# Late projections of an attention kernel: from f32 matmuls to three products of f16 terms

## The reference

```python
xn = _layernorm(x)
q = split(xn @ q_w.T + q_b) / sqrt(16); k = split(xn @ k_w.T + k_b); v = split(xn @ v_w.T + v_b)
attn = softmax(q @ k^T)                  # over all 4096 keys, in float32
att  = merge(attn @ v) @ out_w.T + out_b
w_fp8, w_scale = quant_fp8(weight); x_fp8, x_scale = quant_fp8(xn)
ffn  = (x_fp8 @ w_fp8.T * (x_scale * w_scale) + bias).astype(bfloat16)
out  = x + att + ffn
```

## Time and profile before

| | |
|---|---|
| median of three runs | 1831.96 us |
| the profiled execution | 1832.19 us, span 1830.3 us |
| ACT busy | 1734.1 us, 95% |
| PE busy, DVE busy | 1631.1 us, 1622.4 us (89% each) |
| POOL busy | 48.2 us, 3% |
| exponentials on ACT (line 916) | 1856, busy 1711.1 us |
| matmuls of late projections (line 1632) | 128 records, busy 36.2 us |
| granted TensorE clock | 9 tenths or more of full speed in all 40 slices |

### The profile page before, as it was taken

The page is one execution under the profiler, slowest core; times in us unless marked ns, Lnnn a source line. Parts: engine busy times, 40 slices in busy tenths (PEclk is TensorE's granted clock), DMA queues, the critical chain, the costliest instruction groups (busy, mean ns, idle before and its releaser), DMA issues.

```text
span 1830.3 us, 74852 instructions
## 1 busy us (share of the span) xinstructions
PE 1631.1 (89%) x33478; PEld 558.8 (31%) x33478; DVE 1622.4 (89%) x1876; ACT 1734.1 (95%) x1898; POOL 48.2 (3%) x71
## 2 busy tenths in 40 slices
PE   7998999899899889899888889898898989899887
PEld 4532222222222222222222222222222222222224
DVE  8889989899898989989888998989899898989988
ACT  2499999999999999999999999999999999999993
POOL 0000000000000000000000000000000000000000
PEclk9999999999999999999999999999999999999999
DMA  7401111110111111011110101101000100100113
GB/s 206 143 17 39 36 39 39 32 34 14 42 36 34 44 31 26 23 42 36 34 32 16 35 19 30 25 17 33 21 21 15 25 19 16 27 15 15 31 26 113
DMA packets 127081, 68.59 MB, mean 37 GB/s; under 512 B 77792, under 2 KB 117664, under 8 KB 126752
## 3 DMA queue, kind: packets, MB, share of 16 engines
q1 hardware_dynamic: 126272, 63.54, 13.3%
q10 hardware_dynamic: 480, 0.20, 0.0%
HBM read 41.93 MB, written 17.27 MB: 32 GB/s over the span
## 4 chain that ended last, share of the span: by engine, by line
ACT 45%; issue 26%; PE 18%; DVE 9%; DMA 0%; ACTq 0%; SPq 0%; DVEq 0%
ACT probs L916 45%; PE banks L1666 8%; PE banks L1610 4%; DVE bits L1272 2%; PE banks L1632 2%; PE banks L1521 1%; PE banks L1511 1%; DVE horner L1279 1%; DVE horner L1285 1%; DVE powers L1282 1%; DVE d_probs L1290 1%; PE banks L1793 1%; DVE powers L1276 1%; PE banks L1682 0%; ACTq L915 0%
## 5 line engine op out<-in xcount | busy, mean ns | idle before, releaser
L916 ACT ACTIVATE probs<-banks 128x1024 f32<-128x1024 f32 x1856 | 1711.1, 1116 | 12.4 <-PE banks L1610 5.2
L1666 PE MATMUL banks<-probs,v_st 64*32 64x512 f32 x14848 | 971.1, 590 | 0.3 <-DVEq L1254 0.2
L1610 PE MATMUL banks<-q_st,k_st 50*32 50x512 f16 x16384 | 764.7, 381 | 172.5 <-ACT probs L916 158.0
L1610 PEld LDWEIGHTS banks<-q_st,k_st 50*32 50x32 f16 x16384 | 229.9, 89 | 1070.9 <-ACT probs L916 907.5
L1272 DVE TENSOR_SCALAR bits<-banks 128x1024 int32<-128x1024 f32 x192 | 235.0, 1224 | 64.3 <-PE banks L1610 57.6
L1666 PEld LDWEIGHTS banks<-probs,v_st 64*32 64x32 f32 x14848 | 266.2, 106 | 58.4 <-issue 1.4
L1282 DVE SCALAR_TENSOR_TENSOR powers<-powers,horner 128x1024 f32<-128x1024 int32 x192 | 235.7, 1228 | 6.6
L1279 DVE SCALAR_TENSOR_TENSOR horner<-powers 128x1024 f32<-128x1024 int32 x192 | 235.4, 1226 | 6.6
L1285 DVE SCALAR_TENSOR_TENSOR horner<-powers,horner 128x1024 f32<-128x1024 f32 x192 | 235.2, 1225 | 6.6
L1290 DVE SCALAR_TENSOR_TENSOR d_probs<-horner,bits 128x1024 int32<-128x1024 f32 x192 | 235.2, 1225 | 6.6
L1276 DVE TENSOR_SCALAR powers<-bits 128x1024 int32<-128x1024 int32 x192 | 133.3, 694 | 6.6
(11 more groups left out here) (117 smaller groups left out, 460.4 us busy)
## 6 DMA issues: line engine op xcount, KB each, us to landing
late_x<-xnT_copy SPq DMA_DIRECT2D x32, 256.0 KB, 3.3
k_st<-k_parts SPq DMA_DIRECT2D x96, 64.0 KB, 2.3
q_st<-q_parts SPq DMA_DIRECT2D x186, 32.0 KB, 1.9
k_st<-k_parts SPq DMA_DIRECT2D x96, 60.0 KB, 2.2
xnT_copy<-probs SPq DMA_DIRECT2D x8, 512.0 KB, 3.4
q_st<-neg_row SPq DMA_DIRECT2D x256, 1.0 KB, 1.7
w_f<-xnT_copy SPq DMA_DIRECT2D x16, 256.0 KB, 2.9
xn_all<-ctx_out SPq DMA_DIRECT2D x128, 32.0 KB, 2.2
```

Of the source, the lines that this page charges most:

```text
L916: act.activation(probs[:, at:at + WIDE * CHUNK].rearrange("p (t c) -> p t c", t=WIDE), banks[:, bank:bank + WIDE, :], ACT.Exp, bias=EXP_SHIFT,
L1610: last = pe.matmul(banks[cols, bank + g, :], k_st[rows, keys], blocks[rows, j], start=True, stop=True, tile_position=(g * GROUP, t * VCOLS))
L1666: last = pe.matmul(banks[VCOLS * qb:VCOLS * (qb + 1), 6 + half, :], v_st[keys, kt, :], src[keys, g * CHUNK:(g + 1) * CHUNK], start=at == 0 ...
```

## The change

The late projection is made from f16 terms: x = x_high + x_low and w = w_high + w_low, and the product from w_high x_high, w_high x_low and w_low x_high. With two halves of the 256 input features that is six f16 matmuls in place of two f32 ones.

- ACT writes w_high (f16) instead of the f32 copy, and POOL subtracts it from the weights into w_low, once, before its first copy of values.
- `late_x[:, 0]` is now the one staging buffer of the f32 input, and the memory of `late_x[:, 1]` holds its two f16 terms. POOL makes them, per late projection: a conversion of 128x512 into x_high and a subtraction of 128x512 into x_low (`split_late`). It waits for the load and for the late projection before, which reads the same terms.
- SP loads one input at a time, when the split before has emptied the buffer: slot 0 at the end of the unit before, slot 1 behind the rows of maxima of its own unit.
- POOL's loop over heads is written out, with the splits in front of and between the copies of values.

```diff
+        late_in = late_x[:, 0]
+        late_terms = late_x.rearrange("p i k c -> p i (k c)")[:, 1].bitcast(F16).rearrange("p (t k c) -> p t k c", t=PARTS, k=KD)
...
+        LATE_PRODUCTS = ((0, 0), (0, 1), (1, 0))
...
-            def load_late(n):
+            def load_late(n, slot):
-                for slot in range(len(LATE_AT)):
-                    o, chunk, part = late_item(n * len(LATE_AT) + slot)
-                    at = chunk * CHUNK + part * LATE_COLS
-                    sp.dma_start(late_x[:, slot], xnT_dram[:, :, at:at + LATE_COLS]).then_inc(late_x_in[slot], 16)
+                i = n * len(LATE_AT) + slot
...
+                if i:
+                    sp.wait_ge(late_x_split, i)
+                sp.dma_start(late_in, xnT_dram[:, :, at:at + LATE_COLS]).then_inc(late_x_in, 16)
...
                     save_late(n)
-                    if n + 1 < LATE_UNITS:
-                        load_late(n + 1)
+                    load_late(n + 1, 0)
...
                         load_rows(c, 1, h * 2 + 2)
+                        load_late(h * UNITS, 1)
...
                             load_rows(c, 0, h * 2 + 3)
+                        load_late(h * UNITS + 1, 1)
...
+            pool.wait_ge(late_w_ready, 2)
+            for i, name in enumerate("qk"):
+                high, low = late_w_terms[:, i, 0], late_w_terms[:, i, 1]
+                pool.tensor_tensor(low, w_sb[name][:, :, P:2 * P], high, ALU.subtract).then_inc(late_w_split, 1)
...
+            def split_late(n, slot):
+
+                i = n * len(LATE_AT) + slot
...
+                if i:
+                    h, u = divmod((i - 1) // len(LATE_AT), UNITS)
+                    pool.wait_ge(first.st_done, first.place_0(h, u) + LATE_AT[1 - slot] + 1)
+                pool.wait_ge(late_x_in, 16 * (i + 1))
+                pool.tensor_copy(late_terms[:, 0], late_in).then_inc(late_x_high, 1)
+                pool.wait_ge(late_x_high, i + 1)
+                pool.tensor_tensor(late_terms[:, 1], late_in, late_terms[:, 0], ALU.subtract).then_inc(late_x_split, 1)
...
-                with pool.Fori(1, FIRST_EARLY // UNITS + 1) as h:
-                    head_values(c, h)
+                split_late(0, 0)
+                for n in range(FIRST_EARLY):
+                    split_late(n, 1)
+                    if n % UNITS:
+                        next_values(c, n // UNITS + 1, 0)
+                    split_late(n + 1, 0)
+                    if n % UNITS:
+                        next_values(c, n // UNITS + 1, 1)
...
-                        act.activation(late_w[:, i], w_sb[name][:, :, P:2 * P], ACT.Copy).then_inc(late_w_ready, 1)
+                        act.activation(late_w_terms[:, i, 0], w_sb[name][:, :, P:2 * P], ACT.Copy).then_inc(late_w_ready, 1)
...
-                    pe.wait_ge(late_w_ready, 2)
-                    pe.wait_ge(late_x_in[slot], 16 * (n + 1))
-                    for k in range(KD):
-                        x_cols = late_x[:, slot, k, :]
-                        last = pe.matmul(banks[:, bank_at(h, u, p), 0:LATE_COLS], late_w[:, o, k, :],
+                    pe.wait_ge(late_w_split, 2)
+                    pe.wait_ge(late_x_split, n * len(LATE_AT) + slot + 1)
+                    terms = [(w, x, k) for w, x in LATE_PRODUCTS for k in range(KD)]
+                    for w, x, k in terms:
+                        x_cols = late_terms[:, x, k, :]
+                        last = pe.matmul(banks[:, bank_at(h, u, p), 0:LATE_COLS], late_w_terms[:, o, w, k, :],
                                          x_cols if o else x_cols.rearrange("f (i j p) -> f j i p", i=CT // 2, j=QB),
-                                         start=(k == 0), stop=(k == KD - 1))
+                                         start=(w, x, k) == terms[0], stop=(w, x, k) == terms[-1])
```

More of the change, by code:

```diff
@@ L204, in program @@
         late_w = sb("late_w", [P, 2, KD, P])
+        late_in = late_x[:, 0]
+        late_terms = late_x.rearrange("p i k c -> p i (k c)")[:, 1].bitcast(F16).rearrange("p (t k c) -> p t k c", t=PARTS, k=KD)
+        late_w_terms = late_w.rearrange("p i k c -> p i (k c)").bitcast(F16).rearrange("p i (t k c) -> p i t k c", t=PARTS, k=KD)
         rden_rows = late_x.rearrange("p i k c -> p i (k c)")
@@ L241, in program @@
         late_w_ready = sem("late_w_ready")
-        late_x_in = [sem(f"late_x_in{i}") for i in range(len(LATE_AT))]
+        late_w_split = sem("late_w_split")
+        late_x_in = sem("late_x_in")
+        late_x_high = sem("late_x_high")
+        late_x_split = sem("late_x_split")
         late_hi = sem("late_hi")
@@ L656, in _ @@
             sp.wait_ge(xT_saved, 16 * NCH)
-            def load_late(n):
-                for slot in range(len(LATE_AT)):
-                    o, chunk, part = late_item(n * len(LATE_AT) + slot)
-                    at = chunk * CHUNK + part * LATE_COLS
-                    sp.dma_start(late_x[:, slot], xnT_dram[:, :, at:at + LATE_COLS]).then_inc(late_x_in[slot], 16)
+            def load_late(n, slot):
+                i = n * len(LATE_AT) + slot
+                if n >= LATE_UNITS:
+                    return
+                o, chunk, part = late_item(i)
+                at = chunk * CHUNK + part * LATE_COLS
+                if i:
+                    sp.wait_ge(late_x_split, i)
+                sp.dma_start(late_in, xnT_dram[:, :, at:at + LATE_COLS]).then_inc(late_x_in, 16)
             def save_late(n):
@@ L696, in attend @@
                 else:
-                    load_late(0)
+                    load_late(0, 0)
                 for h in range(HEADS):
@@ L809, in _, with next_values @@
             pool.partition_all_reduce(amax_all[:, :], amax[:, :, 7], P, RMAX).then_inc(amax_shared, 1)
+            def next_values(c, h, half):
+                pool.wait_ge(c.pv_done, h * STEPS + (PV_0 - STEPS) + KT + c.summed[half])
+                copy_values(c, h, half)
             def head_values(c, h):
                 for half in range(2):
-                    pool.wait_ge(c.pv_done, h * STEPS + (PV_0 - STEPS) + KT + c.summed[half])
-                    copy_values(c, h, half)
+                    next_values(c, h, half)
+            def split_late(n, slot):
+                i = n * len(LATE_AT) + slot
+                if n >= LATE_UNITS:
+                    return
+                if i:
[5 more added lines that the diff above has]
+                pool.tensor_tensor(late_terms[:, 1], late_in, late_terms[:, 0], ALU.subtract).then_inc(late_x_split, 1)
             def add_early(h, u, slot):
@@ L1287, in d_block @@
                     dve.wait_ge(c.d_chain, steps + D_STEPS)
+                    if not c.full and h == 0 and u == 0 and n == 0:
+                        dve.wait_ge(late_w_split, 2)
                     if n >= 2:
```

## The result

| | median, us | lowest to highest | runs |
|---|---|---|---|
| before | 1832.13 | 1831.79 to 1833.54 | 5 |
| changed | 1841.25 | 1839.30 to 1842.92 | 5 |

The ratio is 1.0049, with a 95% interval of 1.0035 to 1.0064: the change makes the kernel slower, by 9.1 us. The forecast was 1836.0. The profiled execution of the changed kernel took 1841.14 us (span 1839.3), 9.0 more than that of before.

What follows compares the result with a forecast made beforehand. ACT's own pace was taken as the bound (95% busy). 1832.19 - 9.0 (PE) + 12.8 (POOL's splits) + 0.3 (weights' subtractions) = 1836.3 us profiled, 1836.0 median; range for 8 in 10: 1823 to 1843.

Steps and rivals of the forecast that it cites:

- PE's part: At the 32 late places, six f16 matmuls take 0.77 us instead of 1.06, gaining 9.0 us.
- POOL holds DVE off: DVE's SBUF operations and POOL's exclude each other: a subtraction costs DVE 0.82 us, a conversion 0 to 0.33.
- The split for place 33: At a unit's start it meets DVE's first polynomial; 0.80 us per unit reach ACT, 12.8 us lost over 16 units.
- The delay S of DVE: Time DVE loses to the split at a unit's start: 0.95 us, within 0.2 to 1.15.
- the split for place 63: It meets DVE at the polynomial after place 33, where DVE has idle time: counted 0, upper end 13 us.
- (a): Rival: DVE's delay doesn't reach ACT, 1823.3 us; chance 0.20 in full, 0.14 for half-way cases.
- (c): Rival: PE gains nothing, as an f16 matmul behind a new weight load costs 0.18 us; 1845 us, chance 0.03.
- (d): Rival: the splits are late and PE waits for them; chance 0.02.
- (b): Rival: both splits cost DVE, 6 to 13 us more, 1842 to 1849 us; chance 0.11.

Runs made afterwards that it cites:

- e1: The changed kernel with POOL splitting only the first input, whose terms all 32 late projections use (values wrong): 1823.65 us, -9.0 to before.
- e8: e4 with two products, leaving out that of the weights' low term, so four f16 matmuls per late place: 1823.29 us, -8.4 to before.
- e3: The changed kernel with the load for place 63 issued ahead of the eight loads of rows: 1836.16 us, +3.5 to before.
- e5: The changed kernel with only the input for place 33 loaded earlier and split while DVE reads PSUM: 1828.22 us, -3.5 to before.
- e2: The changed kernel with loads and splits kept, but each late projection two f32 matmuls on other operands (values wrong): 1847.03 us, +14.4 to before.
- e4: e3 plus the load for place 33 issued in the middle of the unit before, split while DVE reads PSUM: 1825.01 us, -7.6 to before.
- e7: e4 with the low by low product as a fourth, so eight f16 matmuls per late place: 1830.27 us, -1.4 to before.
- e6: The changed kernel with POOL only converting, no subtraction, for all inputs but the first (values wrong): 1824.64 us, -7.0 to before.

## Why the prediction was right in sign and short in size

- **PE's part**: right. The late place was forecast at 0.77 us and takes 0.76, and the gain at 9.0 us; e1 shows 9.0. In the sum behind it, a step of 0.08 was set on top of six matmuls of 0.115; e8 has 0.64 for four, where that sum gives 0.54, so it holds at six and not below.
- **POOL holds DVE off**: right, in kind and size. An operation next in line was to lose 0.82 us beside a subtraction, and it loses 0.84. An L1317 that is due just as the subtraction begins loses up to 1.00 (1.69 for 0.69). The conversion was estimated at 0.66 us and takes 0.61 to 0.62. The Trainium skill (SBUF — State Buffer, section "SBUF: two separate sides") has the shared port pair held for a whole instruction; the trace agrees, in that L1320 ends 1.08 us after the subtraction's end, its 1.23 less a start-up that can lie beside it.
- **The split for place 33**: right. The delay S of DVE was put at 0.95 us, and in units 2 to 15 it is 0.96 in the mean (my working from the trace). 0.80 us per unit were forecast to reach ACT, at places 16, 17, 26 and 27. Measured are 10.8 / 15 = 0.72 there and 0.08 at place 37, which e3 and e5 give to the same split: 0.80.
- **The step that failed** is the one on the split for place 63: "PE holds that block's scores back till DVE has freed place 33, in the x24 row from 326.32, so DVE has idle time there; I count 0." The idle time is there, 0.88 us, but it lies ahead of the block, and the load lands behind it, at 329.1. That is the rule and not the exception: of units 1 to 15 only 10, 12 and 14 have the load land so early that the idle time and the PSUM read behind it cover the split. I took idle time somewhere near for cover without working out the landing: the load is issued at 325.52, and with a landing's 3.3 us in the middle that gives 328.8, 0.3 before the block. The conversion began at 329.17 and the subtraction at 329.87, to end at 331.04, and the block reads PSUM only until 330.33. It costs 5.2 us where the sum had 0, in the lower part of the 0 to 13 that the prediction gave for it. So the wide range of 1823 to 1843 held the time, though the sum left this term out.
- **Two gains and losses are not independent**, which no step had: the ACT that gains 0.3 us at the late place has 0.3 less slack at 48, 49. e2 has 1.9 us of stalls there, the changed kernel 5.2, while the split for place 63 held DVE off for 6.4 and 8.0.
- The rest is small. For units 1 to 15 the sum was -8.4 + 12.0 = 3.6 us, and 8.0 were measured: 5.2 more for place 63, 1.0 less for a larger gain on PE (9.4), and 0.2 that I can't place. Units 16 to 30 moved by -0.4, the first stage and unit 0 cancel. The last unit is 1.6 us longer in this profiled execution (56.9 against 55.3). The same 1.1 to 1.6 more stand in e1, e3, e4, e7 and e8, and none in e2, e5 and e6. As e1 has it without splits and e2 has splits without it, it isn't laid to the splits, and what sets it stays open.
- **Rivals.** (a) fell: the delay reaches ACT. (c) and (d) fell: the late place takes 0.76, and PE never waits for a split. (b) was right that the second split costs as well; its lowest price (6) was a little above what came (5.2), and it had 0.11.

## What to carry to other kernels

Work given to an engine that is 3% busy is not free if its operations and those of the engine on which the bound one hangs keep one another waiting: here the price is set by which operation of the neighbour it lies beside, and the same 64 operations of POOL cost 18 us or nearly none (e4) by that alone. For each small operation that a DMA's landing starts, work out the landing time and the neighbour's row at that time; idle time nearby is no cover by itself. And count a gain on the critical engine against the slack of every later wait, since the next wait takes part of it back.

## What the runs showed of the hardware

- The DVE operations that read PSUM and lay beside POOL's were not held off. L1313 takes the same time with POOL beside it as alone, and L1288, which has one input in PSUM and one in SBUF, takes 0.69 us both ways.

```profile
L1313 DVE TENSOR_SCALAR bits<-banks x192: 1160/1225/1226, 85.5 to 1802.5; 128x1024 int32<-128x1024 f32 x192
```

- On POOL, converting 128x512 from f32 to f16 takes 0.61 us, and subtracting f16 from f32 into f16 at the same shape 1.16 us, alone; when they wait for DVE's SBUF work, up to 1.06 and 2.03 in the changed kernel.
- Two f16 matmuls of 256 columns more cost the late place 0.12 us (four to six) and 0.22 us (six to eight), that is 0.06 and 0.11 each. Why the first step is shorter stays open.
